# First cross attention: one softmax instruction over both query tiles of half the heads

## The reference

```python
xn = layer_norm(x, g_x, b_x);  kvn = layer_norm(kv, g_kv, b_kv)
q = heads(xn @ w_q);  k, v = heads(kvn @ w_kv)
attn = einsum('bhqd,bhkd->bhqk', q, k) * SCALE
attn = where(mask == 0, MASK_FILL, attn)
attn = softmax(attn, axis=-1)              # maximum, subtract, exp, sum, divide
out = einsum('bhqk,bhkd->bhqd', attn, v) @ w_proj + b_proj
x = layernorm(x + out)
```

## Time and profile before

| | |
|---|---|
| median of 3 runs | 3854.36 us (3852.84 to 3854.54) |
| the profiled execution: its own time | 3851.82 us |
| its span, first to last instruction | 3850.0 us |
| mean granted TensorE clock | 0.947 of full speed |
| first cross attention in the span | about 340 to 824 us |
| busy share of the span | PE 86%, DVE 82%, ACT 72%, POOL 69% |

### The profile page before, as it was taken

How to read it: one execution, slowest core, us unless ns; L and a number is a source line. 1 busy time by engine, 2 the same in 40 slices (tenths; PEclk the granted TensorE clock), 3 DMA queues, 4 the chain that set the end, 5 groups by cost and what they waited for, 6 DMA issues and landing times. The chain is left out here.

```text
span 3850.0 us, 75338 instructions
## 1 busy us (share of the span) xinstructions
PE 3303.3 (86%) x23328; PEld 2503.5 (65%) x23360; DVE 3137.9 (82%) x5227; ACT 2770.0 (72%) x5061; POOL 2650.3 (69%) x2987
## 2 busy tenths in 40 slices
PE   8996988979964688888888888888898869997887
PEld 5664666667442467677767667767676757775565
DVE  5665899955395798999898989999899949998887
ACT  2223787844475888888888888888888837776887
POOL 1222677730095799999898998999998936665676
PEclk9997999979976899999999999999999989998999
DMA  2111122251112111111111111111111112322121
GB/s 65 54 54 54 42 52 53 50 114 38 44 44 73 43 50 55 56 47 55 48 51 55 56 49 51 51 51 57 55 48 50 53 43 63 78 55 66 50 61 44
DMA packets 285550, 209.63 MB, mean 54 GB/s; under 512 B 131416, under 2 KB 249752, under 8 KB 285224
## 3 DMA queue, kind: packets, MB, share of 16 engines
q1 hardware_dynamic: 285224, 205.72, 19.7%
HBM read 149.18 MB, written 51.41 MB: 52 GB/s over the span
## 5 line engine op out<-in xcount | busy, mean ns | idle before, releaser
L2896 POOL TENSOR_TENSOR ma_ch<-ma_h,ma_crep 128x512 f32<-128x512 f32 x1024 | 1371.0, 1361 | 161.2 <-DVE ma_h L2998 148.0
L2998 DVE TENSOR_TENSOR_SCAN ma_h<-ma_a,ma_pbu 128x512 f32<-128x512 f32 x1024 | 1212.4, 1206 | 174.8 <-PE ma_pbu L2576 113.9
L2576 PE MATMUL ma_pbu<-ma_ident,ma_bu 128*128 128x128 f32 x4096 | 659.9, 285 | 199.2 <-DVE ma_h L2998 158.9
L2576 PEld LDWEIGHTS ma_pbu<-ma_ident,ma_bu 128*128 128x128 f32 x4096 | 480.0, 144 | 441.9 <-DVE ma_h L2998 313.6
L2783 ACT ACTIVATE ma_a<-ma_dt,ma_A 128x510 f32<-128x510 f32 x1024 | 653.2, 717 | 2.0 <-issue 2.0
L2585 PE MATMUL ma_py<-ma_ident,ma_ch 128*128 128x128 f32 x4096 | 627.5, 279 | 0.8 <-POOL ma_ch L2896 0.8
L2774 ACT ACTIVATE ma_bu<-ma_uT,ma_b_t 128x512 f32<-128x512 f32 x784 | 508.0, 718 | 17.1 <-PE ma_pbu L2576 15.3
L2585 PEld LDWEIGHTS ma_py<-ma_ident,ma_ch 128*128 128x128 f32 x4096 | 498.2, 146 | 1.3 <-POOL ma_ch L2896 1.3
L1576 POOL TENSOR_TENSOR xa_prob<-xa_e,xa_rec_head 128x616 f32<-128x616 f32 x128 | 155.7, 1218 | 125.7 <-DVE xa_rec_head L1668 113.6
L924 POOL TENSOR_TENSOR xa_prob<-xa_e,xa_rec_head 128x616 f32<-128x616 f32 x128 | 155.7, 1217 | 108.0 <-DVE xa_rec_head L1016 89.5
L362 POOL TENSOR_TENSOR la_veps<-la_mv,la_eps 128x2 f32<-128x2 f32 x32 | 6.3, 197 | 249.6 <-DVE la_mv L395 249.6
(11 more groups left out here) (375 smaller groups left out, 8007.3 us busy)
## 6 DMA issues: line engine op xcount, KB each, us to landing
ma_crep<-ma_ct_dram SPq DMA_DIRECT2D x256, 256.0 KB
xa_x<-act SPq DMA_DIRECT2D x64, 256.0 KB, 2.8
act<-xa_y SPq DMA_DIRECT2D x64, 256.0 KB, 2.2
la_x<-in_x SPq DMA_DIRECT2D x32, 256.0 KB, 2.8
act<-la_y SPq DMA_DIRECT2D x32, 256.0 KB
act<-ea_x SPq DMA_DIRECT2D x32, 256.0 KB, 4.0
ma_x<-act SPq DMA_DIRECT2D x16, 512.0 KB, 4.6
ma_xr<-act SPq DMA_DIRECT2D x16, 512.0 KB
```

Of the source, the lines that this page charges most:

```text
L2576: last = pe.transpose(pbu[c % 2][:, t * P:(t + 1) * P], bu[:, s % 2, t, c * P:(c + 1) * P], ident[:, :])
L2896: pool.tensor_tensor(ch[:, s % 2, c], h[:, s % 2, c], crep[:, s % 4, :], ALU.mult).then_inc(multiplied, 1)
L2998: dve.tensor_tensor_scan(out=h[:, s % 2, c, :], data0=a[:, s % 2, c, :], data1=pbu[c % 2][:, :], initial=0.0, op0=ALU.mult, op1=ALU.add).t ...
```

## The change

Maximum, subtraction, exponential, sum and reciprocal, which worked on one unit (616 numbers a row), now work on both query tiles of a half of the heads at once: 1232 numbers a row, 16 heads' values. `unit` becomes `pair`, and `expo` and `sums` take the half c in place of the unit u. There are half as many instructions of each kind. `low` has one buffer in place of two; `e`, `esum` and `rec_head` have one for each half. The product on POOL stays one unit in size, but reads its query tile out of the pair's buffers, with a stride between the four groups of two heads. PE's instructions and their order are the same. On ACT the exponential of the pair stands where that of its first unit stood, and that of its second unit is gone from its place. On DVE the maximum and subtraction of the first half of the next batch have moved ahead of the statistics of n-2, and the sum now stands behind the residual.

```diff
@@ -501,7 +501,7 @@
         v_blocks = sb("v_blocks", [P, 2, C, HB, 2, W])
-        top = sb("top", [P, 2, HC])
-        low = sb("low", [P, 2, HC * CTX])
-        e = sb("e", [P, 2, HC * CTX])
-        esum = sb("esum", [P, 2, HC])
-        rec_head = sb("rec_head", [P, 4, HC])
+        top = sb("top", [P, C, T * HC])
+        low = sb("low", [P, T * HC * CTX])
+        e = sb("e", [P, C, T * HC * CTX])
+        esum = sb("esum", [P, C, T * HC])
+        rec_head = sb("rec_head", [P, C, T * HC])
         prob = sb("prob", [P, 2, BL * P])
@@ -561,2 +561,5 @@
 
+        def pair_number(j, b, c):
+            return (4 * C) * j + (C * b + c)
+
         def unit_number(j, b, u):
@@ -680,3 +683,3 @@
                 if not (type(j) is int and j == 0 and b == 0 and c == 0):
-                    pe.wait_ge(low_ready, unit_number(j, b, T * c))
+                    pe.wait_ge(low_ready, pair_number(j, b, c))
                 for t in range(T):
@@ -817,8 +820,8 @@
 
-            def expo(j, b, u):
-                m = unit_number(j, b, u)
+            def expo(j, b, c):
+                m = pair_number(j, b, c)
                 act.wait_ge(low_ready, m + 1)
                 if not (type(m) is int and m < 2):
-                    act.wait_ge(p_ready, m - 1)
-                act.activation(e[:, u % 2], low[:, u % 2], ACT.Exp).then_inc(e_ready, 1)
+                    act.wait_ge(p_ready, T * m - T)
+                act.activation(e[:, c], low[:, :], ACT.Exp).then_inc(e_ready, 1)
 
@@ -839,3 +842,3 @@
                 turned(j, b, 0)
-                expo(j, b, 2)
+                expo(j, b, 1)
                 if nxt is not None:
@@ -846,3 +849,2 @@
                     copy_q(*nxt)
-                expo(j, b, 3)
                 if not normed and nxt is not None:
@@ -859,4 +861,2 @@
                     expo(*nxt, 0)
-                if not normed and nxt is not None:
-                    expo(*nxt, 1)
                 turned(j, b, 3)
@@ -864,4 +864,2 @@
                     copy_x(*after)
-                if normed and nxt is not None:
-                    expo(*nxt, 1)
 
@@ -900,3 +898,2 @@
             expo(0, 0, 0)
-            expo(0, 0, 1)
             copy_x(0, 1)
@@ -920,7 +917,9 @@
                 m = unit_number(j, b, u)
-                pool.wait_ge(rec_head_ready, m + 1)
+                pool.wait_ge(rec_head_ready, pair_number(j, b, u // T) + 1)
                 if not (type(m) is int and m < 2):
                     pool.wait_ge(eT_made, 2 * m - 2)
-                pool.tensor_tensor(prob[:, u % 2, 0:HC * CTX].rearrange("p (h s) -> p h s", h=HC), e[:, u % 2].rearrange("p (h s) -> p h s", h=HC),
-                                   rec_head[:, u, :].unsqueeze(2).broadcast_to([P, HC, CTX]), ALU.mult).then_inc(p_ready, 1)
+                pool.tensor_tensor(prob[:, u % 2, 0:HC * CTX].rearrange("p (g h s) -> p g h s", g=4, h=2),
+                                   e[:, u // T].rearrange("p (g t h s) -> p g t h s", g=4, t=T, h=2)[:, :, u % T],
+                                   rec_head[:, u // T].rearrange("p (g t h) -> p g t h", g=4, t=T)[:, :, u % T].unsqueeze(3).broadcast_to([P, 4, 2, CTX]),
+                                   ALU.mult).then_inc(p_ready, 1)
 
@@ -1001,31 +1000,26 @@
 
-            def unit(j, b, u):
+            def pair(j, b, c):
 
-                dve.wait_ge(scores_made, 2 * number(j, b) + (u // T + 1))
-                s = pS[:, :, u % T, 0:2 * CTX].rearrange("p g (h s) -> p g h s", h=2)
-                m = top[:, u % 2, :].rearrange("p (g h) -> p g h", g=4)
+                dve.wait_ge(scores_made, pair_number(j, b, c) + 1)
+                s = pS[:, :, :, 0:2 * CTX].rearrange("p g t (h s) -> p (g t) h s", h=2)
+                m = top[:, c, :].rearrange("p (k h) -> p k h", h=2)
                 link(dve.tensor_reduce(m, s, AX.X, ALU.max))
-                dve.tensor_tensor(low[:, u % 2].rearrange("p (g h s) -> p g h s", g=4, h=2), s,
-                                  m.unsqueeze(3).broadcast_to([P, 4, 2, CTX]), ALU.subtract).then_inc(low_ready, 1)
+                dve.tensor_tensor(low[:, :].rearrange("p (k h s) -> p k h s", h=2, s=CTX), s,
+                                  m.unsqueeze(3).broadcast_to([P, 4 * T, 2, CTX]), ALU.subtract).then_inc(low_ready, 1)
 
-            def sums(j, b, u):
+            def sums(j, b, c):
 
-                m = unit_number(j, b, u)
-                dve.wait_ge(e_ready, m + 1)
-                link(dve.tensor_reduce(esum[:, u % 2, :], e[:, u % 2].rearrange("p (h s) -> p h s", h=HC), AX.X, ALU.add))
-                dve.reciprocal(rec_head[:, u, :], esum[:, u % 2, :]).then_inc(rec_head_ready, 1)
+                dve.wait_ge(e_ready, pair_number(j, b, c) + 1)
+                link(dve.tensor_reduce(esum[:, c, :], e[:, c].rearrange("p (h s) -> p h s", h=T * HC), AX.X, ALU.add))
+                dve.reciprocal(rec_head[:, c, :], esum[:, c, :]).then_inc(rec_head_ready, 1)
 
             def batch(this, nxt, after, before, two_before, three_before):
-                unit(*this, 2)
-                unit(*this, 3)
-                sums(*this, 2)
+                pair(*this, 1)
                 if after is not None and normed:
                     norm_stats(*after)
-                sums(*this, 3)
+                sums(*this, 1)
+                if nxt is not None:
+                    pair(*nxt, 0)
                 if two_before is not None:
                     moments(*two_before)
-                if nxt is not None:
-                    unit(*nxt, 0)
-                    unit(*nxt, 1)
-                    sums(*nxt, 0)
                 if before is not None:
@@ -1033,3 +1027,3 @@
                 if nxt is not None:
-                    sums(*nxt, 1)
+                    sums(*nxt, 0)
 
@@ -1054,3 +1048,3 @@
 
-            link = Chain(dve, dve_chain, 4 * (2 * U + 2 + normed))
+            link = Chain(dve, dve_chain, 4 * (2 * C + 2 + normed))
             dve.memset(ones[:, :], 1.0)
@@ -1075,6 +1069,4 @@
                     norm_stats(0, b)
-            unit(0, 0, 0)
-            unit(0, 0, 1)
+            pair(0, 0, 0)
             sums(0, 0, 0)
-            sums(0, 0, 1)
             batches(dve, batch, link)
```

## The result

| | before | after |
|---|---|---|
| median of 5 runs each, us | 3852.84 | 3916.50 |
| lowest to highest, us | 3848.14 to 3854.54 | 3909.83 to 3921.34 |
| profiled execution (span) | 3851.82 (3850.0) | 3921.34 (3919.6) |
| first cross attention, first to last instruction | 485.4 (335.8 to 821.3) | 540.2 (335.0 to 875.3) |
| the rest of the span | 3364.6 | 3379.4 |

The ratio is 1.0168, 95% interval [1.0154, 1.0181]: 1.7% slower, 63.7 us by the medians, against 3912 predicted.

The account below looks back on a forecast made before the run. One closed chain through PE, DVE, ACT and POOL was taken as the bound. Its lengthening, 31.7 us, plus 29.9 for clock falls made 61.6 on 3851.8, 3913.4, kept as 3912; range 3870 to 3935.

Parts of the forecast that it names:

- The chain and its terms: First cross attention, scores to next scores through all four engines: period 14.84 us against a mean of 13.85.
- rival 4: POOL's strided product is dear: 0.64 us more a batch, 20 us, 3934 with clock falls; chance 0.03.
- 3.66 and 6.63: Chain terms in us, claimed unchanged: scores' end to exponential, and PE's transposes to the next scores' end.
- The chain's share: Loss from the longer period in the first cross attention: 0.99 us a batch, 31.7 over 32 batches.
- The maximum and subtraction hidden: On DVE the pair starts right behind the scores and ends at 2.9 to 3.2, before the exponential's 3.66.
- the backlog of 0.27: DVE's late work, costing 0.27 us a batch on top of the chain before; claimed to go.
- The residual and statistics not in the way: DVE is free at 4.5 to 4.8, before the exponential ends at 4.92, so the sum does not wait.
- PE's gaps and the clock: PE's waits grow to about 1.1 and 1.3 us; clock falls in 20 of 32 batches, 1.66 each, 29.9 more.
- The sum: Longer chain 31.7 plus clock falls 29.9 gives 61.6 us on the profiled execution's 3851.8.
- Rival 2: DVE is the bound and the change frees it: 1.1 us a batch, 35 in all, 3817; chance 0.05.
- Rival 3: PE is the bound and the longer steps vanish in its slack: 3852; chance 0.05.

Follow-up runs that it names:

- e6: Changed kernel plus ten constant products per batch on PE (5 and 5) in its two waits, results unused; 3876.46 us, ratio 1.0072.
- e7: Kernel before plus four constant products per batch on PE (2 and 2) in the same two waits; 3850.00 us, ratio 1.0001.
- e1: Kernel before with only maximum and subtraction paired, ahead of the statistics of n-2; exponential, sum and reciprocal by units; 3886.96 us, ratio 1.0100.
- e2: Changed kernel with sums and reciprocals by units again; maximum, subtraction and exponential stay paired; 3868.15 us, ratio 1.0046.
- e4: Changed kernel with the pair's sum ahead of the residual on DVE again, as before the change; 3911.46 us, ratio 1.0161.
- e9: Kernel before, unpaired, with POOL making the product of the first half's first tile twice, once into an unread spare tile; 3906.18 us, ratio 1.0157.
- e5: Changed kernel with the first half by units again, the second half all paired, and orders on DVE, ACT and POOL changed; 3845.82 us, ratio 0.9990.
- e10: e5 with POOL's residual factors moved behind the second half's products and DVE's residual statistics split; 3839.05 us, ratio 0.9969.
- e8: Kernel before with only the second half's maximum and subtraction paired, nothing else moved; 3870.02 us, ratio 1.0055.

## Why the prediction was right

- *The chain and its terms.* Predicted 14.84, measured 14.80: exponential 1.22 (1.26), sum to reciprocal 1.47 (1.49), reciprocal 0.25 (0.25), the strided product 1.20 to 1.22 (1.22, so rival 4 is out), 3.66 and 6.63 unchanged. The chain's share was forecast at 31.7, and measured 31.4 in the trace and 33.5 between the stages of e6 and e7.
- *The maximum and subtraction hidden.* Right in the changed kernel: they start 0.08 behind the scores, end 2.99 behind them, and the backlog of 0.27 is gone. But the reason given, PE's and ACT's 3.66, is only half of it. e1 shows the same pair on the path where exponentials and sums by units make it start 1.4 late. In e2 it starts 0.08 behind the scores again, with the sums still by units, so the paired exponential is enough for that.
- *The residual and statistics not in the way.* Right, by the 0.03 between exponential and sum, by DVE's 0.27 of idle time there, and by e4.
- *PE's gaps and the clock.* The gaps were forecast at 1.1 and 1.3 and are 1.08 and 1.33. The falls were forecast in 20 of 32 batches and came in 20 of 31 periods, 1.66 each. That they follow from the waits is shown by e6 (waits filled, no falls) and e9 (waits made by something else, falls). The share itself was the middle between two bounds and not derived; that it fitted so well is luck. The gain over before was mis-sized: 29.9 forecast, 23.0 measured, since the kernel before had four falls in its 31 periods and not two, three of them 6.8 us long and dearer (2.3 to 3.2). The two windows of the earlier trace rows hold one of the three; the other two lie at the stage's start, outside both.
- *The sum.* 61.6 was forecast for the stage, and it grew by 54.8. The profiled executions differ by 69.5 and the medians by 63.7; the remainder lies in parts that the change doesn't touch. Over the twelve profiles, before and after among them, that rest of the span ranges from 3354 to 3379, and after's is the largest; e4 and e9, whose stages are as long as after's, have 3374 and 3359. The state-space layer alone, between the first products of TensorE in it and in the part behind it, ranges from 1891.7 to 1908.2, and after's is again the largest. So part of the agreement of 3912 with 3916.5 is chance, and why the rest varies stays open.
- *Rival 2, DVE as the bound.* Out: DVE was busy 0.78 us a batch less (the rival had put 1.1 on it, from the instructions' own lengths), and the stage took 11% longer. On this point the Trainium skill, page Perfetto Trace Analysis, section Optimizing Scalar/DVE Operations, has a rule for grouping on a saturated engine and one for breaking up where engines that aren't saturated cause bubbles on others. The trace agrees with the second, although DVE was 90% busy: PE's two waits grew from 1.17 to 2.41 us a batch with the joined instructions, and the kernel got slower.
- *Rival 3.* Out: PE's two waits went from 1.17 to 2.41 a batch.

## What to carry to other kernels

Before two instructions are joined, ask when the first part of the result is needed: a joined one delivers its first half only at its end. Where a closed chain through several engines sets the pace, as here, look for the place in which an instruction's result is waited for at once, and leave it by parts there. Joining elsewhere cost nothing here once the orders had been changed with it (e5, e10), but e8, which joined maximum and subtraction there without that, lost 0.55%. When a wait of TensorE grows, price the clock too: of the 54.4 us by which the periods grew, 23.0 were the clock.

## What the runs showed of the hardware

- Ten constant products of 96 columns a batch, 2.65 us of work, went with a granted clock of 1.00 where it had been 0.93, and made the changed kernel some 37 us faster. On the kernel before, whose waits are half as long, four such products changed nothing that can be told.
- A product on POOL whose operand has a stride between groups of 154 numbers costs what the contiguous one costs (1.20 to 1.22 for 616).
- For 1232 numbers in place of 616, DVE takes on average 1.42 to 1.44 in place of 0.78 to 0.80 (maximum out of PSUM, subtraction and sum alike), ACT 1.22 for 0.71, and the reciprocal of 16 takes 0.25, that of 8 0.20. Joining two saves some 0.15 to 0.20 each time; of the long ones, the first tile's result comes 0.51 to 0.64 later.
